# Two graph layers on one core: wider one-hot operations, a second product in halves, and a block transpose in place of a TensorE transpose

## The chip, the cores and the metric

The kernel runs on one core of one Trainium2 chip. The metric is the device time of one execution in microseconds (us). TensorE is PE in the profile, its weight loads are PEld, VectorE is DVE, ScalarE is ACT, GpSimd is POOL, and SyncE (SP) issues most DMAs.

## The reference, cut to what matters

There are 1250 nodes and 40000 edges, sorted by `dst`, with 512 features each.

```python
h = relu(layernorm(x))
msg = (h[src] + edge_attr) @ Wm.T + bm
agg = segment_sum(msg, dst) / max(deg, 1)
out = h + gelu(concat(h, agg) @ Wu.T + bu)
x = x + layernorm(out) * gamma + beta
h = relu(layernorm(x))
neigh = segment_sum(h[src], dst)
x = x + relu(((1 + eps) * h + neigh) @ W1 + b1) @ W2 + b2 + h
```

## The kernel before, in words

The sum over edges is made before the product with Wm. It has two parts: the sum of `edge_attr` rows per node, and the sum of `h[src]` per node, which is a product of h with a matrix of counts (how many edges go from node s to node d).

**The stream.** The 40000 edges are cut into 79 groups of 512 (NG = 79, the last has 64). SP loads each group (1 MB) into one of four buffers `ea` and reuses a buffer when `sums_done` says that the group's products are complete. Within a group there are two halves of 256 edges. As the edges are sorted, the nodes of a half lie in a window of W = 22 columns, whose first column is read at run time (`offsets`, two windows a group).

**Step n of the loop on PE** does, in this order: `sums(n)`, `turn(n-1)`, `counts(m)` for one or two groups m (`COUNTS`, four counts in three steps, so that all 79 are counted at step FULL = 58), then what `ASIDE` has for that step: a product of weights, a transpose of h0 (`T_AT`, one 128-row block each) or `u1` (`U_AT`, the product of a transposed block of h0 with Wu1T, four 128x512 matmuls in float32, which the profile shows as eight records). From step PIECE_AT = 60 on there is a `piece` in every step: eight matmuls of 512 columns that multiply the high part Hh and the low part Hl of h0 by a converted block of counts (ARc).

- `sums(n)` multiplies one-hot matrices oneD (512 edges by 22 columns) with `ea`. It uses four column groups of the PE array side by side: a 22-column weight sits at rows 0, 32, 64 or 96 of the output. It is 8 matmuls of 256 columns, 16 records.
- `turn(n)` transposes the packed sums. ACT copies them out of PSUM (`packed_copy`), PE transposes two blocks of 128x128, and the turned sums are then added into aggT. Before step EARLY = 59 ACT copies them again (`turned_copy`) and POOL adds (L400). From EARLY on DVE adds them straight from PSUM (L680).
- `counts(m)` multiplies the one-hot matrices oneS and oneK (bf16): four matmuls of 220 columns into one of two banks. DVE adds that bank into A16 (L669, `add_counts`, two halves). `counts(m)` waits until the adds of m-2 are complete.

**Step n on DVE** is an order written by hand: `sums_hots(n+2)` (oneD, two buffers, so it waits until `sums(n)` is complete), then for each counted group m: add of half 0, `key_hots(m+2)` (oneK, L648), add of half 1, `source_hots(m+2)` (oneS, L648). Then come the add of turned sums (from step 60 on), the drain of u1 (L688), folds of A16 (L698, steps 59 to 63), the degrees (step 66) and `has_bias` (steps 67 to 76). At step OUT_AT = 70 it drains the first ten pieces (`piece_out`, L720), and the eleventh piece on PE waits for that.

**POOL** adds the turned sums of groups 0 to 58 and makes the low part of h0, `low_h0` (L386: Hl = X - Hh), ten operations in steps T_AT + 2 (6 to 17). ACT makes the high part in the same steps (`HH_AT`). The first `piece` waits for all ten low parts.

After the loop come the rest of the pieces, `map_agg`, the first layer's normalisation, the second layer's products with the counts (L1171, L1172), the hidden layer (L1245) and the output (L1260). The change does not touch this part, except that the statistics of the second normalisation go to the array `stats` of the first.

Of the kernel before, what the change touches and what calls it, by code (L numbers as in the profile page):

```python
# [14 lines left out]
P = 128  # L15
SUB = 4
SLOTS = 4
HOTS = 2
# [9 lines left out]
def gnn_kernel(nc, x, src, dst, edge, Wm, bm, Wu, bu, gamma, beta, W1, b1, W2, b2, eps, out):  # L28
# [34 lines left out]
    assert len(ASIDE) == 4 + 2 * NT and U_AT[-1] < FULL and GEN_AT not in ASIDE and GEN_AT - 1 not in ASIDE  # L63
# [11 lines left out]
    DEG_BANK = 2 + (DEG_AT - 1) % 2  # L75
# [31 lines left out]

    stream_at = at[0]
    ea = [place(f"ea{s}", [P, SUB, D], F32)[0] for s in range(SLOTS)]
    oneD = [place(f"oneD{s}", [P, SUB, W], F32)[0] for s in range(HOTS)]  # L110
    oneS = [place(f"oneS{s}", [P, 2, P, 2], BF16)[0] for s in range(HOTS)]
    oneK = [place(f"oneK{s}", [P, 2, KW, 2], BF16)[0] for s in range(HOTS)]
    turned_sums = [place(f"turned_sums{s}", [P, D // 2], F32)[0] for s in range(HOTS)]
    packed_sums = [place(f"packed_sums{s}", [P, D // 2], F32)[0] for s in range(HOTS)]
# [5 lines left out]
    assert stream_at + NT * NP * 4 <= arc_at + NT * 256 * 4  # L120

    g_names = ["dst_f", "srel", "big", "valid", "hi_f", "lo_f", "key", "tmp"]
    dst_f, srel, big, valid, hi_f, lo_f, key, tmpf = [place("g_" + name, [P, GE], F32, arc_at + n * GE * 4)[0] for n, name in enumerate(g_names)]
    dst_i, _ = place("dst_i", [P, GE], I32, arc_at + 8 * GE * 4)
    src_i, _ = place("src_i", [P, GE], I32, arc_at + 9 * GE * 4)
    genE, _ = place("genE", [P, SUB, D], F32, arc_at)
    genD, _ = place("genD", [P, SUB, P], F32, arc_at + SUB * D * 4)
    genS, _ = place("genS", [P, SUB, P], BF16, arc_at + SUB * D * 4 + SUB * P * 4)
    genK, _ = place("genK", [P, SUB, P], BF16, arc_at + SUB * D * 4 + SUB * P * 6)

    idx_at = -(-at[0] // 32) * 32
    idxT = {n: place("T_" + n, [P, SUB, GP], F32)[0] for n in ("srel", "lo", "hi", "dE", "hit")}
# [3 lines left out]
    assert TB * 2048 <= 5 * SUB * GP * 4  # L136
    h0t = [place(f"h0t{i}", [P, D], F32)[0] for i in range(TB)]
    iotaF, _ = place("iotaF", [P, P], F32)
# [25 lines left out]
    stats2, _ = place("stats2", [P, NT, 6], F32)  # L164
# [12 lines left out]
    with ctx:  # L177
# [14 lines left out]
        counts_done = sem("counts_done")  # L192
        counts_zero = sem("counts_zero")
# [30 lines left out]
        turned_out = sem("turned_out")  # L224
# [17 lines left out]
        packed_out = sem("packed_out")  # L242
# [18 lines left out]
        turned = sem("turned")  # L261
        u1_done = sem("u1_done")
# [94 lines left out]
        def _(pool):  # L357
# [30 lines left out]
            def add_sums_of(n):  # L388
# [3 lines left out]
                for half, first in enumerate((loaded[0] & 0xFFFF, loaded[0] >> 16)):  # L392
# [6 lines left out]
                    sums = turned_sums[n % HOTS][:].rearrange("p (f q) -> p f q", f=FC)[:, :, half * QUAD:half * QUAD + W]  # L399
# [44 lines left out]
        def _(act):  # L444
# [62 lines left out]
            for n in range(NG):  # L507
                packed_copy(n)
# [26 lines left out]
            act.wait_ge(turned, NG)  # L535
# [54 lines left out]
        def _(dve):  # L590
# [45 lines left out]
            def sums_hots(n):  # L636
                if n >= HOTS:
                    dve.wait_ge(sums_done, n - HOTS + 1)
                n1 = idxT["srel"][:, :, n:n + 1].broadcast_to([P, SUB, W])
                V.tensor_tensor(oneD[n % HOTS][:], iotaF[:, 0:W].rearrange("p (a n) -> p a n", a=1).broadcast_to([P, SUB, W]), n1,  # L640
                                ALU.is_equal).then_inc(hotD_ready, 1)

            def counts_hots(m, hot, width, name, ready):
                if m >= HOTS:
                    dve.wait_ge(counts_done, m - HOTS + 1)
                iota = iotaP[:, 0:width].rearrange("p (a c) j -> p a c j", a=1).broadcast_to([P, 2, width, 2])
                mine = pairT[name][:, m].rearrange("p h (a j) -> p h a j", a=1).broadcast_to([P, 2, width, 2])
                V.tensor_tensor(hot[m % HOTS][:], iota, mine, ALU.is_equal).then_inc(ready, 1)  # L648

            def key_hots(m):  # L650
                counts_hots(m, oneK, KW, "key", hotK_ready)

            def source_hots(m):
                counts_hots(m, oneS, P, "lo", hotS_ready)
# [15 lines left out]

            def add_sums_of(n, half, first):
                cols = aggT[:, :, bass.ds(first, W)]
                if half == 0:
                    dve.wait_ge(turned, n + 1)
# [4 lines left out]
                sums = ps[:, 2 + n % 2, 0:256].rearrange("p (f q) -> p f q", f=FC)[:, :, half * QUAD:half * QUAD + W]  # L679
# [64 lines left out]
            for n in range(NG):  # L744
                if n + HOTS < NG:
                    sums_hots(n + HOTS)
# [541 lines left out]
```

## Time and profile before

| | us |
|---|---|
| three runs | 528.18, 529.69, 530.55 |
| median | 529.69 |
| the profiled execution, its own time | 526.39 |
| its span, first to last instruction | 524.6 |
| PE busy in the span | 482.8 (92%) |
| DVE busy | 283.0 (54%) |
| ACT busy | 147.5 (28%) |
| POOL busy | 166.8 (32%) |

Busy shares are means over stages that have different limits, so they are to be read stage by stage. All times below are from the start of the span. The loop's first `sums` starts at 27.75 us, and the loop's step 60, the first with a piece, begins at 208.53 us.

### The profile page before, as it was taken

The numbers are of one execution on the slowest core, as the hardware profiler recorded it, in microseconds if no ns is written. First come the engines' busy times: TensorE is split into PE (matmuls) and PEld (weight loads), VectorE is DVE, ScalarE is ACT, GpSimd is POOL, SyncE is SP. The second block draws the span as 40 slices with busy tenths as digits, with TensorE's granted clock in tenths as the row PEclk, the third lists the DMA queues.
The fourth block names the chain that finished last, engine by engine and source line by source line (L and its number), as shares of the span: only waits on it lengthen the run. The fifth ranks groups of instructions, "written<-read, shape, count | busy, mean of one in ns | idle before, by whom it ended". The sixth has DMA issues, their size and how long they took to land.

```text
span 524.6 us, 8826 instructions
## 1 busy us (share of the span) xinstructions
PE 482.8 (92%) x3003; PEld 277.0 (53%) x3003; DVE 283.0 (54%) x660; ACT 147.5 (28%) x291; POOL 166.8 (32%) x217
## 2 busy tenths in 40 slices
PE   5889999898898988999999999599989999999997
PEld 4446554444444544675665655379944446744442
DVE  6897887888777779645434789983000000011111
ACT  4416644123222223222237245441011122100000
POOL 7323665333322224000023267636994000000000
PEclk9999999999999999999999999799999999999999
DMA  8998998889999999988820111112040000011111
GB/s 299 316 367 301 338 327 292 348 342 361 352 367 358 374 363 390 408 308 315 271 82 2 32 29 41 35 62 100 1 163 0 0 0 1 0 41 40 41 40 35
DMA packets 31115, 98.95 MB, mean 189 GB/s; under 512 B 3577, under 2 KB 3577, under 8 KB 31067
## 3 DMA queue, kind: packets, MB, share of 16 engines
q1 hardware_dynamic: 30458, 97.27, 50.7%
q10 hardware_dynamic: 608, 1.05, 0.7%
q8 instruction: 28, 0.46, 0.4%
q14 instruction: 21, 0.16, 0.1%
HBM read 95.76 MB, written 2.56 MB: 187 GB/s over the span
## 4 chain that ended last, share of the span: by engine, by line
PE 63%; DVE 21%; issue 6%; PEld 6%; DVEq 1%; POOL 1%; DMA 1%; SPq 0%; PEldq 0%; POOLq 0%
PE ps L1260 13%; PE ps L1245 13%; PE ps L1007 9%; PE ps L1048 7%; DVE A L669 5%; PE ps L1105 5%; PE ps L1106 4%; PE ps L1018 4%; PE ps L1194 3%; PEld ps L1171 3%; PE ps L1036 3%; PEld ps L1172 2%; DVE U L893 2%; DVE tt L871 2%; DVE oneS L648 2%
## 5 line engine op out<-in xcount | busy, mean ns | idle before, releaser
L400 POOL TENSOR_TENSOR aggT<-turned_sums,aggT 128x88 f32 x118 | 53.9, 456 | 107.4 <-ACT turned_sums L473 94.4
L1007 PE MATMUL ps<-ea,oneD 128*22 128x256 f32 x1264 | 83.9, 383 | 1.4 <-DVE oneD L640 0.9
L947 DVE TENSOR_TENSOR U<-ps,U 128x512 f32<-128x512 f32 (+1 forms) x10 | 6.9, 692 | 130.8 <-PE ps L1260 130.8
L467 ACT COPY packed_sums<-ps 128x256 f32<-128x256 f32 x79 | 29.4, 372 | 163.9 <-PE ps L1007 163.9
L1245 PE MATMUL ps<-aggT,W1s 128*128 (+1 forms) x192 | 67.4, 513 | 2.2 <-PEq L1239 2.2
L1260 PE MATMUL ps<-W2s,hid 128*128 128x512 f32 (+1 forms) x160 | 68.8, 592 | 0.0
L669 DVE TENSOR_TENSOR A<-ps,A 128x220 f32 x158 | 60.3, 381 | 8.6 <-PE ps L1018 8.0
L1018 PE MATMUL ps<-oneK,oneS 128*128 128x220 bf16 x316 | 42.5, 259 | 14.7 <-DVE oneS L648 13.0
L1245 PEld LDWEIGHTS ps<-aggT,W1s 128*128 128x128 f32 x192 | 36.4, 190 | 33.1 <-issue 33.0
L1007 PEld LDWEIGHTS ps<-ea,oneD 128*22 128x22 f32 x1264 | 30.5, 101 | 41.1 <-issue 23.6
L648 DVE TENSOR_TENSOR oneK<-iotaP,P_key 128x880 bf16<-128x880 bf16 x79 | 51.8, 655 | 0.0
L1260 PEld LDWEIGHTS ps<-W2s,hid 128*128 128x128 f32 (+1 forms) x160 | 30.0, 188 | 38.2 <-issue 38.2
L1171 PE MATMUL ps<-AR,Hh 128*128 128x256 f32 (+1 forms) x160 | 45.2, 318 | 0.5
L1172 PE MATMUL ps<-AR,Hl 128*128 128x256 f32 (+1 forms) x160 | 44.0, 312 | 0.0
L640 DVE TENSOR_TENSOR oneD<-iotaF,T_srel 128x88 f32<-128x88 f32 x79 | 22.4, 283 | 37.0 <-PE ps L1007 35.8
L1018 PEld LDWEIGHTS ps<-oneK,oneS 128*128 128x128 bf16 x316 | 28.9, 97 | 21.2 <-DVE oneK L648 11.7
L648 DVE TENSOR_TENSOR oneS<-iotaP,P_lo 128x512 bf16<-128x512 bf16 x79 | 39.2, 496 | 0.0
L1194 PE MATMUL ps<-CT,aggT 128*128 128x512 f32 x80 | 36.0, 593 | 1.2 <-DVE aggT L720 1.2
L581 ACT ACTIVATE hid<-ps,b1C 128x512 f32 (+1 forms) x24 | 14.6, 608 | 80.3 <-PE ps L1245 80.3
L1048 PE MATMUL ps<-Wu1T,U 128*128 128x512 f32 x80 | 36.1, 593 | 0.0
L1036 PE MATMUL ps<-ident,packed_sums 128*128 128x128 f32 x158 | 34.5, 300 | 0.0
L1105 PE MATMUL ps<-ARc,Hh 128*128 128x512 f32 x80 | 33.4, 417 | 1.0 <-DVE aggT L720 1.0
(139 smaller groups left out, 645.1 us busy)
## 6 DMA issues: line engine op xcount, KB each, us to landing
ea<-in_edge_attr_dram SPq DMA_DIRECT2D x78, 1024.0 KB, 7.6
X<-in_x_dram SPq DMA_DIRECT2D x1, 2304.0 KB
xt<-in_x_dram SPq DMA_DIRECT2D x9, 256.0 KB, 2.7
out_dram<-U SPq DMA_DIRECT2D x9, 256.0 KB
W1s<-in_L_gnn_W_dram SPq DMA_DIRECT2D x1, 2048.0 KB, 7.7
W2s<-in_L_gnn_W_dram SPq DMA_DIRECT2D x1, 2048.0 KB, 8.7
WuN<-in_L_gnn_Wu_dram ACTq DMA_DIRECT2D x1, 1024.0 KB, 5.4
WuN<-in_L_gnn_Wu_dram SPq DMA_DIRECT2D x1, 1024.0 KB, 6.8
```

The lines of the kernel that those rows point to most:

```text
L400: nc.gpsimd.tensor_tensor(cols, sums, cols, ALU.add).then_inc(early_step, 1)
L648: V.tensor_tensor(hot[m % HOTS][:], iota, mine, ALU.is_equal).then_inc(ready, 1)
L669: V.tensor_tensor(cols, ps[:, 4 + m % 2, half * KW:(half + 1) * KW].rearrange("p (h w) -> p h w", w=W), cols, ALU.add).then_inc(add_step, 1)
L1007: last = T.matmul(to.rearrange("p (c d) -> p c d", c=2), oneD[h][:, g * 2 + j, :], data, start=j == 0, stop=j == 1)
L1018: last = T.matmul(ps[:, 4 + m % 2, (j // 2) * KW:(j // 2 + 1) * KW], oneS[h][:, j // 2, :, j % 2], oneK[h][:, j // 2, :, j % 2], start=j % ...
L1048: last = T.matmul(ps[:, ASIDE_BANK["u1", b], :], U[:, b, f * P:(f + 1) * P], Wu1T[:, f, :], start=f == 0, stop=f == FC - 1)
L1105: T.matmul(to, Hh[:, c, rows], counted, start=c == 0 and (q < 2 or f % 2 == 0), stop=False)
L1171: T.matmul(to, Hh[:, b, rows], AR[:, b, start:start + cols], start=b == 0 and (cols == 512 or f % 2 == 0), stop=False)
L1172: last = T.matmul(to, Hl[:, b, rows], AR[:, b, start:start + cols], start=False, stop=b == NT - 1 and (cols == 512 or f % 2 == 1))
L1194: last = T.matmul(ps[:, 2 + b % 2, :], aggT[:, f, b * P:(b + 1) * P], CT[:, f, :], start=f == 0, stop=f == FC - 1)
L1245: last = T.matmul(ps[:, CHUNK_BANK[k % 4], 0:cols], W1s[:, f, k * P:(k + 1) * P], aggT[:, f, bass.ds(start, cols)], start=f == 0, stop=f = ...
L1260: last = T.matmul(ps[0:rows, 6 + b % 2, :], hid[:, k, b * P:b * P + rows], W2s[:, k, :], start=k == 0, stop=k == KC - 1)
```

## The change

1. **u1 in two halves.** `u1(b)` makes its first two products at step U_AT[b] and the other two at the next step, and DVE drains it one step later. U_AT is 7, 12, 17, ..., 52 now; T_AT is more spread.
2. **One-hots of two groups per operation.** `pair_hots` makes oneK (and another one oneS) of the groups 2p and 2p+1 at once, in one of three pair buffers. At an even m the keys of the pair m//2 + 2 are made between the two adds, at an odd m the sources of that pair. oneD has three buffers, so `sums_hots(n+2)` in step n waits for `sums(n-1)` only.
3. **Low parts late.** `HH_AT` is 55 to 64 in place of 6 to 17, for ACT's high parts and POOL's low parts. A piece waits for its own low part alone.
4. **Block transposes.** From group EARLY = 59 on (20 groups) PE makes no `turn`, and ACT no `packed_copy`. `sums` puts each 32-column block of features where a transpose of 32x32 blocks turns it right: 16 matmuls of 128 columns in place of 8 of 256. DVE transposes the bank from PSUM to SBUF (`turn_blocks`, 128x256 float32) and then adds from SBUF. PE's `sums(n)` waits for `blocks_turned` of n-2. The products for the degrees come at step 65, after `sums`, and no longer inside `turn`.
5. Buffers are placed anew: two of the three pair buffers lie in the space of ARc, which is free until the counts are complete.

```diff
-HOTS = 2
+HOTS = 3
+SUM_HOTS = 3
+TURNS = 2
-    T_AT = [4, 5, 6, 8, 9, 10, 11, 13, 14, 15]
-    U_AT = [7, 12, 16, 21, 26, 32, 37, 42, 47, 52]
-    HH_AT = [t + 2 for t in T_AT]
+    T_AT = [4, 5, 6, 10, 11, 15, 16, 20, 21, 25]
+    U_AT = [7, 12, 17, 22, 27, 32, 37, 42, 47, 52]
+    HH_AT = [FULL - 3 + b for b in range(NT)]
...
+            def pair_hots(p, hot, width, name, ready):
+                if p >= HOTS:
+                    dve.wait_ge(counts_done, 2 * (p - HOTS + 1))
+                groups = min(2, NG - 2 * p)
+                halves_of = 2 * groups
+                iota = iotaP[:, 0:width].rearrange("p (a c) j -> p a c j", a=1).broadcast_to([P, halves_of, width, 2])
+                mine = pairT[name][:, 2 * p:2 * p + groups].rearrange("p g h (a j) -> p (g h) a j", a=1).broadcast_to([P, halves_of, width, 2])
+                V.tensor_tensor(hot[p % HOTS][:, 0:groups].rearrange("p g h c j -> p (g h) c j"), iota, mine, ALU.is_equal).then_inc(ready, 1)
...
+            def turn_blocks(n):
+                dve.wait_ge(sums_done, n + 1)
+                if n < TURNS + EARLY:
+                    dve.wait_ge(early_step, (n - TURNS + 1) * 2)
+                else:
+                    dve.wait_ge(sum_step, (n - TURNS + 1 - EARLY) * 2)
+                V.transpose(turned_sums[n % TURNS][:], ps[:, n % 2, 0:D // 2]).then_inc(blocks_turned, 1)
...
             for n in range(NG):
-                if n + HOTS < NG:
-                    sums_hots(n + HOTS)
                 if n > EARLY:
+                    turn_blocks(n - 1)
                     sum_first = offsets(n - 1)
+                if n > 0 and n - 1 + SUM_HOTS < NG:
+                    sums_hots(n - 1 + SUM_HOTS)
                 for m in COUNTS[n]:
                     first = count_first
                     add_counts(m, 0, first[0])
-                    if m + HOTS < NG:
-                        key_hots(m + HOTS)
+                    ahead = m // 2 + HOTS - 1
+                    if m % 2 == 0 and ahead < PAIRS:
+                        key_hots(ahead)
+                    elif ahead < PAIRS:
+                        source_hots(ahead)
                     if m + 1 < NG:
                         count_first = offsets(m + 1)
                     add_counts(m, 1, first[1])
-                    if m + HOTS < NG:
-                        source_hots(m + HOTS)
...
-                    elif kind == "u1":
-                        u1(k)
+                if n - 2 in U_AT:
+                    u1(U_AT.index(n - 2))
...
             def sums(n):
...
-                if n >= 2:
+                if 2 <= n < EARLY + 2:
                     pe.wait_ge(packed_out, n - 1)
+                elif n >= 2:
+                    pe.wait_ge(blocks_turned, n - 1 - EARLY)
...
+                else:
                     for g in range(2):
+                        for j in range(2):
+                            data = ea[s][:, g * 2 + j, :].rearrange("p (k q e) -> p q k e", k=FC, q=FC)
+                            for q in range(FC):
+                                to = ps[q * QUAD:q * QUAD + W, n % 2, g * P:(g + 1) * P]
+                                last = T.matmul(to.rearrange("p (k e) -> p k e", k=FC), oneD[h][:, g * 2 + j, :], data[:, q],
+                                                start=j == 0, stop=j == 1)
...
-                if n > 0:
+                if 0 < n <= EARLY:
                     turn(n - 1)
+                if n == DEG_AT - 1:
+                    degree_products()
                 for m in COUNTS[n]:
                     counts(m)
+                if n - 1 in U_AT:
+                    u1(U_AT.index(n - 1), 2)
```

## Rows read from the trace of the kernel before

**Rows 1.** Windows: span, then PE, PEld, DVE, ACT, POOL busy (x), clock, DMA share, GB/s

```profile
27.70:206.20 178.50, 161.99 (x1521) 84.78 (x1520) 148.59 (x400) 60.16 (x151) 67.49 (x125) 1.00 0.93 347
200.00:220.00 20.00, 18.14 (x183) 10.51 (x173) 16.20 (x42) 6.76 (x17) 3.93 (x9) 1.00 1.02 408
206.20:276.60 70.40, 67.33 (x544) 42.02 (x543) 35.50 (x93) 21.01 (x49) 6.44 (x8) 1.00 0.77 279
```

**Rows 2.** Chain of waits in the first stage: start us, us, what (x records)

```profile
174.75 3.45 PE ps L1048 x8
...
187.84 0.99 PE ps L1007 x16
188.84 0.37 PE ps L1036 x2
189.20 0.40 PE ps L1018 x4
189.60 3.45 PE ps L1048 x8
```

**Rows 3.** Waits in 60 to 200 us: total us, times, longest

```profile
DVE oneD L640 <- PE ps L1007: 17.1, 9, 2.6
...
PE ps L1018 <- DVE oneS L648: 10.6, 13, 1.4
PEld ps L1018 <- DVE oneK L648: 10.5, 9, 1.6
```

**Rows 4.** Timeline of DVE in a stretch where it has fallen behind: start us, us

```profile
121.07 0.39 DVE L669 TENSOR_TENSOR A<-ps,A 128x220 f32 x1
121.37 0.61 DVE L648 TENSOR_TENSOR oneK<-iotaP,P_key 128x880 bf16<-128x880 bf16 x1
...
122.19 0.42 DVE L648 TENSOR_TENSOR oneS<-iotaP,P_lo 128x512 bf16<-128x512 bf16 x1
122.52 0.69 DVE L688 TENSOR_TENSOR U<-ps,buB 128x512 f32<-128x512 f32 x1
```

**Rows 5.** A low part on POOL at 62.79 us, and DVE's one-hot beside it

```profile
62.79 1.26 POOL L386 TENSOR_TENSOR Hl<-X,Hh 128x512 fp32r<-128x512 f32 x1
...
62.85 1.49 DVE L648 TENSOR_TENSOR oneS<-iotaP,P_lo 128x512 bf16<-128x512 bf16 x1
```

**Rows 6.** The stream's loads: landing time, and issues on SP

```profile
DMA to landing us min/median/max: 2.3/7.6/13.6
...
SPq L312 <- PE ps L1007: 204.7, 74, 7.5
```

**Rows 7.** Chain of waits in the late steps, 239 to 251 us

```profile
240.69 0.37 PE ps L1036 x2
241.06 0.24 PE ps L1105
...
242.90 1.04 PE ps L1007 x16
...
243.97 0.25 DVE oneD L640
...
244.41 0.70 DVE aggT L720
...
247.68 0.99 PE ps L1007 x16
```

**Rows 8.** Weight loads by line, ns min/median/max; then one row of the chain

```profile
L1007 PEld LDWEIGHTS ps<-ea,oneD x1264: 97/102/103, 27.8 to 270.5; 128*22 128x22 f32 x181
...
L1018 PEld LDWEIGHTS ps<-oneK,oneS x316: 96/97/100, 28.7 to 205.9; 128*128 128x128 bf16 x158
...
67.18 0.44 PE ps L1042 x4
```

**Rows 9.** Timeline of DVE in a step with folds

```profile
212.87 0.25 DVE L640 TENSOR_TENSOR oneD<-iotaF,T_srel 128x88 f32<-128x88 f32 x1 [0.33 <-PE ps L1007]
213.47 0.25 DVE L680 TENSOR_TENSOR aggT<-ps,aggT 128x88 f32 x1 [0.36 <-PE ps L1036]
...
214.07 1.68 DVE L698 TENSOR_TENSOR acc<-acc,A 128x1280 uint16<-128x1280 uint16 x2
```

More of the change, by code:

```diff
@@ L62, in gnn_kernel @@
     GEN_AT = 29
-    assert len(ASIDE) == 4 + 2 * NT and U_AT[-1] < FULL and GEN_AT not in ASIDE and GEN_AT - 1 not in ASIDE
+    assert len(ASIDE) == 4 + 2 * NT and U_AT[-1] + 2 < FULL and GEN_AT not in ASIDE and GEN_AT - 1 not in ASIDE
     EARLY = FULL + 1
@@ L106, in gnn_kernel @@
     xt = [place(f"xt{i}", [P, D], F32, w1_at + i * 2048)[0] for i in range(TB)]
+    PAIRS = -(-NG // 2)
     stream_at = at[0]
     ea = [place(f"ea{s}", [P, SUB, D], F32)[0] for s in range(SLOTS)]
[L110 to L114, printed above, removed]
+    oneD = [place(f"oneD{s}", [P, SUB, W], F32)[0] for s in range(SUM_HOTS)]
+    packed_sums = [place(f"packed_sums{s}", [P, D // 2], F32)[0] for s in range(TURNS)]
+    turned_sums = [place(f"turned_sums{s}", [P, D // 2], F32)[0] for s in range(TURNS)]
+    oneK = [place("oneK0", [P, 2, 2, KW, 2], BF16)[0]]
     at[0] = -(-at[0] // 64) * 64
@@ L408, in _ @@
                         low_h0(b)
+            for b in range(NT):
+                if HH_AT[b] >= EARLY:
+                    low_h0(b)
             pool.wait_ge(low0_ready, NT)
@@ L723, in _ @@
             dve.wait_ge(consts, 3)
-            for n in range(HOTS):
+            for n in range(SUM_HOTS):
                 sums_hots(n)
-                key_hots(n)
-                source_hots(n)
+            for p in range(HOTS - 1):
+                key_hots(p)
+                source_hots(p)
             dve.wait_ge(x_in, 32)
@@ L825, in _ @@
                         V.nop()
+            turn_blocks(NG - 1)
             sum_first = offsets(NG - 1)
@@ L1009, in sums @@
                 last.then_inc(sums_done, 1)
             def counts(m):
-                h = m % HOTS
-                pe.wait_ge(hotK_ready, m + 1)
-                pe.wait_ge(hotS_ready, m + 1)
+                sources, keys = [t[m // 2 % HOTS][:, m % 2] for t in (oneS, oneK)]
+                pe.wait_ge(hotK_ready, m // 2 + 1)
+                pe.wait_ge(hotS_ready, m // 2 + 1)
                 if m >= 2:
@@ L1017, in counts @@
                 for j in range(SUB):
-                    last = T.matmul(ps[:, 4 + m % 2, (j // 2) * KW:(j // 2 + 1) * KW], oneS[h][:, j // 2, :, j % 2], oneK[h][:, j // 2, :, j % 2],
+                    last = T.matmul(ps[:, 4 + m % 2, (j // 2) * KW:(j // 2 + 1) * KW], sources[:, j // 2, :, j % 2], keys[:, j // 2, :, j % 2],
                                     start=j % 2 == 0, stop=j % 2 == 1)
@@ L1043, in transpose_h0, with u1 @@
                 last.then_inc(hT_mm, 1)
-            def u1(b):
+            def u1(b, first):
                 pe.wait_ge(hT_done, b + 1)
-                for f in range(FC):
+                for f in range(first, first + 2):
                     last = T.matmul(ps[:, ASIDE_BANK["u1", b], :], U[:, b, f * P:(f + 1) * P], Wu1T[:, f, :], start=f == 0, stop=f == FC - 1)
-                last.then_inc(u1_mm, 1)
+                if first == 2:
+                    last.then_inc(u1_mm, 1)
             def bank_free(what):
@@ L1103, in piece @@
                     to = bank("D", f, cols) if q == 2 else ps[:, 4 + f, 0:cols]
-                    counted = (ARd if q == 2 else ARc)[:, c, :]
-                    T.matmul(to, Hh[:, c, rows], counted, start=c == 0 and (q < 2 or f % 2 == 0), stop=False)
-                    last = T.matmul(to, Hl[:, c, rows], counted, start=False, stop=c == NT - 1 and (q < 2 or f % 2 == 1))
+                    here = (ARd if q == 2 else ARc)[:, c, :]
+                    T.matmul(to, Hh[:, c, rows], here, start=c == 0 and (q < 2 or f % 2 == 0), stop=False)
+                    last = T.matmul(to, Hl[:, c, rows], here, start=False, stop=c == NT - 1 and (q < 2 or f % 2 == 1))
                 last.then_inc(piece_mm, 1)
```

125 lines of the change are left out of this document (65 added, 60 removed).

## The prediction

> **What bounds the kernel now.** I read the windows first, to split the span into stages. The loop's steps 0 to 58 take the 178.5 us from 27.7 to 206.2, and the late steps, in which each has a piece, end at 276.6 [rows 1]. Behind 276.6 nothing of weight is changed. The reader is to see that no engine is full in the first stage: PE is busy for 162.0 us, DVE for 148.6, and the DMA moves 347 GB/s. In the late stage PE is busy for 67.3 of 70.4 us.
>
> Then the chain of waits gives PE's own price list [rows 2]: `sums` 0.99, `turn` 0.37, `counts` 0.40, `u1` 3.45, and a block's transposes 0.44 [rows 8]. The first stage by that list: 59 x 0.99 = 58.4, 58 x 0.37 = 21.5, 79 x 0.40 = 31.6, 10 x 3.45 = 34.5, two products of weights as long as a u1 = 6.9, ten transposes 4.4 and some 0.9 for two index tables: 158.2 us. So PE stands still for 20.3 of the 178.5 us. The waits name the cause: PE waits for oneS and oneK, 13 and 10 times in 140 us (10.6 and 10.5 us, partly the same time), while DVE for its part waits 17.1 us for `sums` [rows 3]. Two engines that wait for each other in turn are coupled too tightly. DVE waits while PE works off a u1 (between two u1 there are 14.85 us, from 174.75 to 189.60 [rows 2]), and then it is the slower one: a count costs it 1.45 us (121.07 to 122.52 [rows 4]), against 0.40 on PE.
>
> The loads are not the limit now: `ea` lands 7.6 us after issue in the median, SP spends 204.7 us waiting for a free buffer [rows 6], and PE never waits for `ea` [rows 3].
>
> **Early steps: u1 in halves, pairs.** Five steps hold one u1 and 6.67 counts. PE: 5 x (0.99 + 0.37) + 6.67 x 0.40 + 3.45 = 12.9 us, so of the 14.85 us 1.9 are stall. DVE: 6.67 x 1.45 = 9.7, 5 x 0.35 for oneD with its gap (0.25 [rows 9]) = 1.8, and the drain of u1 0.6: 12.1 us. In a step with one count DVE needs 1.8 us and PE 1.76, in one with two DVE 3.3 and PE 2.16. With 1.67 such steps, the drain and small change DVE falls back by some 2.8 us in five steps. A u1 gives it 3.45 us to catch up, but only a lag of about 1 us can be carried, since PE is never more than two counts ahead: the stall is 2.8 - 1.0 = 1.8, as measured. What does the change do to this?
> - Pairs. A key operation takes 0.52 us to the next start, a source operation 0.33 [rows 4], for 880 and 512 elements: 0.52 ns an element and 0.06 us fixed. A pair operation then takes 0.98 or 0.60 us, and saves 0.06. That is 0.12 us a pair, 0.4 us in five steps. With two counts in a step the add of the second now follows the add before it directly, with a gap of 0.18 as between two adds [rows 9]: 0.3 back. So pairs give DVE almost nothing.
> - Deeper buffers. A count on PE waits for the sources of m now, made directly after the add of m-2. It will wait for that add itself, which the code demands in both kernels. At even m the add now stands behind a key operation of 0.98 in place of 0.52, at odd m behind 0.60. Together no gain.
> - u1 in halves gives two breaks of 1.7 us, one step apart. The first takes up the lag carried, the second some of the next step's. I put the lag that is left over the other steps at 2.2 us, the stall at 1.2, and the gain at 0.7 us in five steps, 7 us over ten u1. The ends are 0, if two bursts so close act as one, and 1.9 x 10 = 19, if every stall goes.
>
> **Low parts.** A low part on POOL takes 1.26 us, and a one-hot that starts beside it takes 1.49 instead of 0.42 [rows 4, 5]: 1.07 us of DVE for each of ten, at most 10.7. They leave steps 6 to 17, where DVE is late anyway. I take 3 us of PE time (bounds 0, if other stalls take their place, and 6, a little over half of the 10.7). At the seam, PE begins step 60 at 208.53, 2.32 us after step 59 at 206.21, where its work is 1.36: DVE was late with oneD. The third oneD buffer takes this wait away, the conversion for the first piece stays behind the last count: 0.5 us. Early gain: 7 + 3 + 0.5 = 10.5 us.
>
> DMA: 10.5 us less in 59 steps is 2.85 us a step for 1.05 MB, 368 GB/s, and a window around the seam has 408 GB/s [rows 1], so I see no wait.
>
> **Late steps: the turn goes.** From the end of `sums` to the first piece there are 0.37 us (240.69 to 241.06 [rows 7]). Some of it is the way from packed to full-width matmuls and stays, so I take 0.28 a group. `sums` becomes eight rounds of 128 columns in place of four of 256. Four transposes of 128 columns take 0.44, 0.11 each [rows 8], and eight of those are 0.88, four rounds now take 0.99 with their start: I add 0.05. Net 0.23 x 20 = 4.6 us. The bounds of the round: it can't be shorter than now (0), and if each load of weights (0.102 us [rows 8]) had to end before the next round could stream, eight rounds would take 8 x 0.21 = 1.68, 0.7 more. I keep near the first: without overlap the four rounds of now would take 4 x (0.102 + 0.22) = 1.29, and 0.99 is measured.
>
> The Trainium skill says otherwise ("TensorE: Matmul & The Clock Gate", Part 3, The mechanism): weight loads overlap running matmuls only when the row group differs. Here all weights use all 128 rows, so by that rule nothing would overlap; the 0.99 us disagree with it at 256 columns, and no row shows 128 in column groups. By the rule the late steps would come out as in the second rival.
>
> Step 70: from 242.90 to 247.68 it takes 4.78 us, 1.57 more than the others (3.21), because `piece_out` (first at 244.41) starts only after the oneD operation at 243.97, which waits for that step's `sums` [rows 7]. With three buffers DVE starts about 1 us earlier: 1.0 us gained.
>
> **DVE in the late steps.** The block transpose isn't in the trace. Between 0.25 us for 88 columns and 0.69 for 512 [rows 4, 9] a line gives 0.42 for 256, and that is my value; bounds 0.25 and 1.0. In a fold step DVE has 0.42 + 0.25 + 0.50 + 1.68 and gaps of 0.4, 3.25 us, against PE's new 2.98. That makes it late by 1.4 us in five steps. Six low parts now fall into these steps and can block a fold each, 1.07 x 6 = 6.4 us. Behind the block transpose waits PE's `sums` of the next but one group: the leeway is two steps less one `sums`, 5.0 us. So up to 2.8 us of stall; I take 1.0, as low parts can meet idle time. With a transpose of 1.0 us it is up to 5.7. After step 64 DVE needs at most 0.42 + 0.25 + 0.50 + 0.7 + 0.4 = 2.3 us a step and is covered. ACT loses its copy. POOL ends its sums later by four low parts (5 us), and DVE's first add of its own waits for that, inside the same leeway.
>
> Late gain: 4.6 + 1.0 - 1.0 = 4.6 us.
>
> **The sum.** 10.5 + 4.6 = 15.1 us from 526.39, the profiled execution's own time (span 524.6 and 1.79 around it): 511.3. The median of the runs is 3.30 above that execution, and I keep the distance: 514.6.
>
> **The rivals.**
> - *Early steps hardly gain* (0.18). The add stands behind a longer operation and two bursts act as one: only the low parts and late steps pay, 3 + 0.5 + 4.6 = 8.1, so 522. For it: DVE's work per count is all but unchanged, 12.1 against 12.9 us. Against it: both have slack by that sum.
> - *Loads bind the narrow rounds* (0.10). 20 x 0.7 = 14 us against 5.6: late steps lose 8.5 to 9.5 us, with the early 10.5 it gives 528.5, no difference that can be told. Against it: the overlap seen now.
> - *Every stall goes* (0.06): 19 + 0.5 early, 4.6 late: 505.5. Against it: the loads would have to run at 1.05 MB in 2.7 us, 390 GB/s, with four buffers.
> - *Slower* (0.08): the pair operation with its four-part pattern runs at half the rate per element. Then a pair of groups costs 2784 x 0.52 = 1.45 us more on DVE, 4.8 us in five steps: DVE 16.9 us against the 14.85 of now, and the first stage is 2.05 x 12 = 24 us longer, 19 after the late gain: 544 to 549. It decides from about 0.85 ns an element on (0.4 us in five steps more than now would eat the late gain). Against it: the innermost pair of elements is laid out as before.
>
> **How the numbers follow.** The forecast has 0.58, with a range of its own from 508 to 520. A measurement here tells 0.5% (2.6 us) from no change. Faster: 0.58 + 0.18 + 0.06 = 0.82; same 0.10; slower 0.08. The range from 505 to 527.5 holds forecast and first rival, and most of the third, and leaves out some 2 in 10.
>
> **What would show it.** Right: waits of PE for one-hots fall from 20.3 us to about 10; one-hots last 1.07 and 0.69 us; no one-hot of 1.49 in steps 6 to 17; late steps 2.98 us apart; step 70 about 3.5; a block transpose of 0.42 us. Wrong: PE waits for the adds in L669's place as long as for one-hots before, rounds 0.2 us apart in `sums`, PE waiting for `blocks_turned` at steps 61 to 66, or PE waiting for `ea`.

## The result, and the profile after

The changed kernel takes 525.33 us (median of 20 runs, 522.43 to 528.55) against 527.89 (20 runs, 526.24 to 530.55). The ratio is 0.9955, with a 95% interval from 0.9938 to 0.9972. It is faster by 0.45%, some 2.4 us, where 15 were forecast. The time lies inside the stated range, but the gain is a sixth of the forecast. The two profiled executions, which all stretches below come from, took 526.39 and 525.55 us and differ by 0.8 us, the medians by 2.6.

The profile gives a span of 523.4 us. The windows of the kernel after, in the stretches of [rows 1]:

```profile
27.70:206.20 178.50, 166.82 (x1597) 87.65 (x1596) 141.89 (x333) 60.72 (x152) 69.89 (x123) 1.00 0.97 359
206.20:276.60 70.40, 65.98 (x757) 47.33 (x756) 48.88 (x107) 15.23 (x32) 17.02 (x13) 0.93 0.70 249
```

In the first stage PE does more in the same time (166.8 us of work against 162.0). In the second the granted clock is 0.93, where it was 1.00, POOL has 17 us of work in place of 6.4, and DVE 48.9 in place of 35.5.

To place the difference I took the start of each step, that is of its first `sums` record, from both traces (us):

| | before | after | after less before |
|---|---|---|---|
| step 0 | 27.75 | 29.45 | +1.70 |
| step 5 | 47.00 | 48.72 | +1.72 |
| step 21 | 97.47 | 93.96 | -3.51 |
| step 58 | 204.46 | 199.58 | -4.88 |
| step 63 | 218.15 | 219.24 | +1.09 |
| step 78 | 270.05 | 269.22 | -0.83 |
| `map_agg` | 276.64 | 274.92 | -1.72 |

At step 58 the new kernel is 4.9 us ahead, and five steps later 1.1 us behind. It loses 6.0 us between 199 and 219 us. The timeline of DVE and POOL there:

```profile
202.58 1.35 POOL L398 TENSOR_TENSOR Hl<-X,Hh 128x512 fp32r<-128x512 f32 x1
202.72 1.89 DVE L724 TENSOR_TENSOR acc<-A 128x1280 uint16<-128x1280 uint16 x1
...
205.45 0.44 DVE L695 STREAM_TRANSPOSE turned_sums<-ps 128x256 f32<-128x256 f32 x1
...
205.73 9.90 POOL L398 TENSOR_TENSOR Hl<-X,Hh 128x512 fp32r<-128x512 f32 x7
205.82 1.32 DVE L656 TENSOR_TENSOR oneD<-iotaF,T_srel 128x88 f32<-128x88 f32 x1
...
207.06 1.32 DVE L706 TENSOR_TENSOR aggT<-turned_sums,aggT 128x88 f32 x1
...
208.56 1.08 DVE L706 TENSOR_TENSOR aggT<-turned_sums,aggT 128x88 f32 x1 [0.18 <-DVE aggT L706]
...
209.56 3.70 DVE L724 TENSOR_TENSOR acc<-acc,A 128x1280 uint16<-128x1280 uint16 x2
...
213.19 0.44 DVE L695 STREAM_TRANSPOSE turned_sums<-ps 128x256 f32<-128x256 f32 x1
213.55 0.94 DVE L656 TENSOR_TENSOR oneD<-iotaF,T_srel 128x88 f32<-128x88 f32 x1
214.42 1.31 DVE L706 TENSOR_TENSOR aggT<-turned_sums,aggT 128x88 f32 x1
...
213.77 1.92 PE L1048 MATMUL ps<-ea,oneD 128*22 128x128 f32 x32 [3.72 <-DVE turned_sums L695]
```

POOL works off seven low parts without a break (9.90 us). Beside them the DVE operations with both inputs in SBUF are longer: oneD takes 1.32 us instead of 0.25, the two adds 1.32 and 1.08 instead of 0.25, two folds 3.70 instead of 1.68 [rows 9]. The block transpose, which reads PSUM alone, takes its 0.44. From one block transpose to the next pass 7.74 us, 5.0 of them lost beside POOL, and PE waits 3.72 us for the second. Within that wait, at about 212.2 us, the clock falls to 1.2 GHz. It stays there for 6.8 us, and the `sums` behind the wait takes 1.92 us where others take 1.07. The wait of 3.72 us and some 5.2 us of work at half clock, which is at most 2.6 us lost by estimate, make up nearly all of the 6.0 us (the turns that went give back 0.4).

### The profile page after: what moved, and what is told of

Its sections match the earlier page's. It is cut to its first block, busy times and chain, and to the rows that moved or that the text cites. A ratio compares the mean times of both kernels' runs of the same rounds, so it can differ in the third digit from the quotient of the medians.

```text
span 523.4 us, 9297 instructions
## 1 busy us (share of the span) xinstructions
PE 484.4 (93%) x3283; PEld 284.5 (54%) x3283; DVE 288.5 (55%) x602; ACT 140.9 (27%) x271; POOL 177.0 (34%) x217
## 4 chain that ended last, share of the span: by engine, by line
PE 65%; DVE 19%; issue 7%; PEld 6%; POOL 1%; DVEq 1%; DMA 1%; SPq 0%; PEldq 0%; POOLq 0%
PE ps L1305 13%; PE ps L1290 13%; PE ps L1040 7%; PE ps L1087 7%; PE ps L1146 5%; PE ps L1147 4%; PE ps L1059 4%; DVE A L687 4%; PE ps L1048 4%; PE ps L1239 3%; PEld ps L1215 3%; PE ps L1068 3%; PEld ps L1216 2%; DVE U L923 2%; DVE tt L901 2%
## 5 line engine op out<-in xcount | busy, mean ns | idle before, releaser
L412 POOL TENSOR_TENSOR aggT<-turned_sums,aggT 128x88 f32 x118 | 63.8, 541 | 101.3 <-ACT turned_sums L488 87.8
L687 DVE TENSOR_TENSOR A<-ps,A 128x220 f32 x158 | 60.7, 384 | 35.8 <-PE ps L1059 25.8
L1040 PE MATMUL ps<-ea,oneD 128*22 128x256 f32 x944 | 62.7, 383 | 0.1
L482 ACT COPY packed_sums<-ps 128x256 f32<-128x256 f32 x59 | 21.9, 372 | 113.5 <-PE ps L1040 113.3
L666 DVE TENSOR_TENSOR oneK<-iotaP,P_key 128x1760 bf16<-128x1760 bf16 (+1 forms) x40 | 42.6, 1066 | 0.0
L1040 PEld LDWEIGHTS ps<-ea,oneD 128*22 128x22 f32 x944 | 22.6, 101 | 35.2 <-issue 15.8
L1087 PE MATMUL ps<-Wu1T,U 128*128 128x512 f32 x80 | 37.8, 595 | 0.0
L1146 PE MATMUL ps<-ARc,Hh 128*128 128x512 f32 x80 | 35.4, 442 | 0.0
L1147 PE MATMUL ps<-ARc,Hl 128*128 128x512 f32 x80 | 33.1, 414 | 0.0
L1215 PEld LDWEIGHTS ps<-AR,Hh 128*128 128x128 f32 x160 | 31.0, 194 | 3.2 <-DVE Hl L944 1.3
L428 POOL TENSOR_TENSOR xt<-xt,betaB 128x512 f32<-128x512 f32 x10 | 14.3, 1429 | 52.7 <-DMA xt<-in_x_dram 52.5
```

Of the source, the lines that this page charges most:

```text
L412: nc.gpsimd.tensor_tensor(cols, sums, cols, ALU.add).then_inc(early_step, 1)
L687: V.tensor_tensor(cols, ps[:, 4 + m % 2, half * KW:(half + 1) * KW].rearrange("p (h w) -> p h w", w=W), cols, ALU.add).then_inc(add_step, 1)
L1040: last = T.matmul(to.rearrange("p (c d) -> p c d", c=2), oneD[h][:, g * 2 + j, :], data, start=j == 0, stop=j == 1)
L1087: last = T.matmul(ps[:, ASIDE_BANK["u1", b], :], U[:, b, f * P:(f + 1) * P], Wu1T[:, f, :], start=f == 0, stop=f == FC - 1)
L1146: T.matmul(to, Hh[:, c, rows], here, start=c == 0 and (q < 2 or f % 2 == 0), stop=False)
L1147: last = T.matmul(to, Hl[:, c, rows], here, start=False, stop=c == NT - 1 and (q < 2 or f % 2 == 1))
```

## The experiments

All but the changed kernel, whose row is the result above, were run in five rounds against the kernel before, which had 527.6 to 528.4 us there. The table gives the ratio to it (95% interval) and stretches of the profiled execution in us, between the starts of steps.

| kernel | us | ratio | steps 0-5 | 5-21 | 21-58 | 58-63 |
|---|---|---|---|---|---|---|
| before | | | 19.25 | 50.47 | 106.99 | 13.69 |
| changed | 525.33 | 0.9955 (0.9938 to 0.9972) | 19.27 | 45.24 | 105.62 | 19.67 |
| a_low_early | 521.40 | 0.9858 (0.9819 to 0.9898) | 20.82 | 46.03 | 105.49 | 13.72 |
| b_low_on_act | 518.35 | 0.9819 (0.9773 to 0.9865) | 19.13 | 45.24 | 104.63 | 13.86 |
| h_turn_psum | 523.87 | 0.9929 (0.9903 to 0.9955) | 19.30 | 45.24 | 105.62 | 16.62 |
| g_low_at_u1 | 521.54 | 0.9879 (0.9845 to 0.9914) | 19.65 | 46.02 | 108.06 | 13.51 |
| i_b_low_late | 523.43 | 0.9917 (0.9884 to 0.9949) | 19.38 | 45.56 | 108.37 | 14.10 |
| j_b_u1_halves | 523.94 | 0.9916 (0.9884 to 0.9948) | 18.33 | 46.15 | 108.05 | 13.44 |
| k_b_block_turn | 524.85 | 0.9942 (0.9916 to 0.9968) | 19.24 | 50.47 | 106.98 | 12.76 |
| l_u1_whole | 528.88 | 1.0013 (0.9985 to 1.0041) | 19.20 | 46.08 | 109.55 | 18.83 |
| m_no_pairs | 524.49 | 0.9944 (0.9918 to 0.9971) | 19.41 | 44.63 | 106.11 | 18.89 |
| n_low_early_start | 518.45 | 0.9815 (0.9788 to 0.9842) | 17.71 | 46.02 | 105.44 | 13.60 |
| p_low_on_dve | 516.17 | 0.9801 (0.9772 to 0.9831) | 17.65 | 45.24 | 104.68 | 12.81 |
| q_b_spread | 534.67 | 1.0142 (1.0118 to 1.0167) | 18.25 | 52.09 | 111.38 | 14.41 |

### Where are the 6 us of the seam?

**a_low_early**

```diff
-    HH_AT = [FULL - 3 + b for b in range(NT)]
+    HH_AT = [t + 2 for t in T_AT]
```

> The changed kernel with the low and high parts of h0 back in steps T_AT + 2 (6 to 27), nothing else. Seam theory: in the changed kernel the ten low parts run on POOL almost without a break from 197 to 216 us, in the steps in which DVE has the folds, and each blocks a DVE operation that reads two SBUF tensors (folds, oneD, the adds, which now read SBUF). PE then waits 3.7 us for a block transpose and its clock is halved for 6.8 us. With the low parts early the wait for blocks_turned and the slow clock at 212 us should be gone, the late steps start 5 to 6 us earlier, early steps lose 1 to 3 us: 521 to 523 us against 525.3. Rival (DVE is too full by the block transposes and the folds alone): the wait for blocks_turned stays above 2 us and the time is 525 to 528.

As expected, 521.40 us. Steps 58 to 63 fall from 19.67 to 13.72 us, and PE has no wait for a block transpose. So DVE is not too full by block transposes and folds alone, and the rival falls. What the early place costs is small: 0.8 us in steps 5 to 21.

**b_low_on_act**, which leaves out the subtraction of the low parts:

```diff
                 nc.scalar.copy(Hh[:, b, :], X[:, b, :]).then_inc(hi0_ready, 1)
+                act.wait_ge(hi0_ready, b + 1)
+                act.wait_ge(hT_mm, b + 1)
+                nc.scalar.activation(Hl[:, b, :], X[:, b, :], ACT.Copy, scale=0.0).then_inc(low0_ready, 1)
...
-                nc.gpsimd.tensor_tensor(Hl[:, b, :], X[:, b, :], Hh[:, b, :].bitcast(F32), ALU.subtract).then_inc(low0_ready, 1)
+                pool.wait_ge(low0_ready, b + 1)
```

> The changed kernel in which the low parts are made by ACT at the same late steps as 0 times X (this leaves the subtraction out, Hl becomes zero), so POOL and DVE don't meet there and all else keeps its place. Seam theory: no operation of DVE longer than its median between 197 and 216 us, no wait of PE for blocks_turned, full clock at 212 us: 6 us less than the changed kernel, 518.5 to 520. Rival (DVE too full by itself): within 1.5 us of the changed kernel's 525.3.

The seam takes 13.86 us with ten ACT operations in the same steps. DVE's timeline is even: a fold step takes 2.85 us (204.64 to 207.49) and nothing is stretched.

```profile
204.64 1.68 DVE L727 TENSOR_TENSOR acc<-acc,A 128x1280 uint16<-128x1280 uint16 x2
206.24 0.44 DVE L698 STREAM_TRANSPOSE turned_sums<-ps 128x256 f32<-128x256 f32 x1
206.60 0.21 DVE L659 TENSOR_TENSOR oneD<-iotaF,T_srel 128x88 f32<-128x88 f32 x1
206.89 0.25 DVE L709 TENSOR_TENSOR aggT<-turned_sums,aggT 128x88 f32 x1
...
207.49 1.68 DVE L727 TENSOR_TENSOR acc<-acc,A 128x1280 uint16<-128x1280 uint16 x2
```

The time, 518.35 us, is a little below what was expected. The cause is shown by this pair of runs: the late place alone costs nothing, it costs when POOL does the work beside these DVE operations. That Hl is zero in this run does not make the seam short, as a_low_early has the true low parts and the same 13.7 us.

**h_turn_psum** writes the block transpose to one PSUM bank, so it also waits for the adds of the group before:

```diff
...
-                V.transpose(turned_sums[n % TURNS][:], ps[:, n % 2, 0:D // 2]).then_inc(blocks_turned, 1)
+                V.transpose(ps[:, 3, 0:D // 2], ps[:, n % 2, 0:D // 2]).then_inc(blocks_turned, 1)
...
-                sums = turned_sums[n % TURNS][:].rearrange("p (h k w) -> p h k w", h=2, w=QUAD)[:, half, :, 0:W]
+                sums = ps[:, 3, 0:D // 2].rearrange("p (h k w) -> p h k w", h=2, w=QUAD)[:, half, :, 0:W]
```

> The changed kernel with the block transpose written to PSUM bank 3 instead of SBUF, so that the adds of the late groups read PSUM and SBUF as before the change. Seam theory in its fuller form: adds that read PSUM are not blocked by POOL (those of the counts never were, 373 to 393 ns), so at the seam only folds and oneD are: DVE regains the 3.0 us that three adds lost, and PE's wait falls from 3.7 to about 1: 522.5 to 524. If adds are blocked whatever they read, or the blocked folds alone decide, no difference: 525.3 within 1 us.

The time, 523.87 us, is as expected, but by the two intervals it can't be told from the changed kernel. What the run shows is in its profile. DVE's timeline:

```profile
205.69 1.31 DVE L656 TENSOR_TENSOR oneD<-iotaF,T_srel 128x88 f32<-128x88 f32 x1
206.93 0.24 DVE L706 TENSOR_TENSOR aggT<-ps,aggT 128x88 f32 x1
207.34 0.25 DVE L706 TENSOR_TENSOR aggT<-ps,aggT 128x88 f32 x1 [0.18 <-DVE aggT L706]
207.51 3.15 DVE L724 TENSOR_TENSOR acc<-acc,A 128x1280 uint16<-128x1280 uint16 x2
210.58 0.45 DVE L695 STREAM_TRANSPOSE ps<-ps 128x256 f32<-128x256 f32 x1
```

And its waits at the seam (total us, times, longest):

```profile
PE ps L1048 <- DVE ps L695: 3.4, 2, 1.8
```

The adds keep their 0.25 us beside running low parts, while oneD and folds are still stretched. The next block transpose starts at 210.58 instead of 213.19, and steps 58 to 63 shrink by 3.05 us. PE still waits 3.4 us for block transposes, but in two pieces, and no half clock follows. So about half the loss at the seam came from moving the source of the adds from PSUM to SBUF, together with the slow clock behind the long wait; this run does not separate the two.

**g_low_at_u1**

```diff
-    HH_AT = [FULL - 3 + b for b in range(NT)]
+    HH_AT = [u + 1 for u in U_AT]
```

> The changed kernel with one low part in each step U_AT + 1 (8, 13, ..., 53), where DVE has idle time while PE works off u1. Seam theory: the seam's 6 us come back, and the 1.07 us that each low part takes from a one-hot falls into DVE's idle time: 519 to 521 us. Rival (a low part costs its 1.07 us of DVE wherever it stands): ten of them cost the early steps what the seam gives back: 524 to 526.

The seam is clean (13.51 us), but steps 21 to 58 take 108.06 us against 105.62, and steps 5 to 21 0.8 us more. Against b_low_on_act steps 5 to 58 are 4.2 us longer, so a low part costs PE 0.4 us there, less than its 1.07 and not nothing. The time lies between the two expectations.

### What is each part worth by itself?

**i_b_low_late**: the kernel before with part 3 alone.

```diff
-    HH_AT = [t + 2 for t in T_AT]
+    HH_AT = [FULL - 3 + b for b in range(NT)]
...
-                    pe.wait_ge(low0_ready, NT)
+                if q == 0:
+                    pe.wait_ge(low0_ready, c + 1)
```

> The kernel before with the low and high parts of h0 moved to steps 55 to 64, nothing else. Seam theory: POOL's run of low parts blocks DVE's folds and oneD here too, but the late adds read PSUM and no product on PE waits for a block transpose, so only oneD (two buffers) can hold PE up: 1 to 3 us lost at the seam. The early steps gain about 0.5 us (what moving them back cost in the run before), more (up to 3 us) if they hurt more where u1 is whole. Time 526 to 530 against 527.6. Rival (the low parts cost nothing unless block transposes are there): 524 to 527.

Better than either theory had it. Steps 5 to 21 gain 4.9 us, steps 21 to 58 lose 1.4 (0.9 of them in steps 53 to 58, where the late low parts begin), and the seam only 0.4, although oneD and folds are stretched here too. The timeline of DVE shows the adds from PSUM at their full speed beside them:

```profile
211.04 1.33 DVE L643 TENSOR_TENSOR oneD<-iotaF,T_srel 128x88 f32<-128x88 f32 x1
212.30 0.24 DVE L683 TENSOR_TENSOR aggT<-ps,aggT 128x88 f32 x1
...
212.88 3.15 DVE L701 TENSOR_TENSOR acc<-acc,A 128x1280 uint16<-128x1280 uint16 x2
```

At the seam the late low parts hurt only where PE also waits for DVE's block transposes.

**j_b_u1_halves**: the kernel before with part 1 alone, **l_u1_whole**: the changed kernel without it, and **q_b_spread**: the kernel before with the new positions and whole u1.

```diff
-    T_AT = [4, 5, 6, 8, 9, 10, 11, 13, 14, 15]
-    U_AT = [7, 12, 16, 21, 26, 32, 37, 42, 47, 52]
+    T_AT = [4, 5, 6, 10, 11, 15, 16, 20, 21, 25]
+    U_AT = [7, 12, 17, 22, 27, 32, 37, 42, 47, 52]
...
-            def u1(b):
+            def u1(b, first):
                 pe.wait_ge(hT_done, b + 1)
-                for f in range(FC):
+                for f in range(first, first + 2):
```

(q_b_spread has the first four lines alone, l_u1_whole the whole edit in reverse.)

> The kernel before with u1 in halves and the new T_AT and U_AT, nothing else (low parts stay at T_AT + 2). If the halves make the early gain (as the prediction has it, 0.7 us in five steps), step 58 starts 5 to 7 us earlier than in the kernel before: 521 to 523 against 527.6. Rival (the halves need the deeper buffers for one-hots to be worth something): gain under 2 us.

> The changed kernel with u1 whole again and the old T_AT and U_AT (part 1 undone). If the halves make the early gain, step 58 starts 4 to 6 us later than in the changed kernel and the time is 529 to 531; the seam stays as it is in the changed kernel. Rival (pairs and deeper buffers make it): step 58 within 1.5 us of the changed kernel's, 525 to 527.

> The kernel before with the new T_AT and U_AT alone: transposes of h0, and with them the high and low parts (T_AT + 2), spread over steps 4 to 27, u1 whole. If the spread and not the halves made the gain of the kernel with both (523.94 us; steps 5 to 21 in 46.2 us against 50.5, steps 21 to 58 in 108.1 against 107.0), this one has 46 to 47 and 107.5 to 109: 524 us. Rival (the halves made it): 49.5 to 50.5 in steps 5 to 21, 526.5 to 528 us.

Halves with their new positions gain 4.4 us by the ratio, and taking both out of the changed kernel costs 3.1 (1.0013 against 0.9955; step 58 starts 4.65 us later). Both are more than the rivals allowed and a little less than was expected. q_b_spread refutes both its theories: with whole u1 the new positions are worse than the old, by 1.4%. Twice in the first stage of its trace the clock is at half, each time from within a wait of PE for oneS on. The rows are the two products that ended these waits, and the windows:

```profile
81.21 0.89 PE L1018 MATMUL ps<-oneK,oneS 128*128 128x220 bf16 x4 [2.59 <-DVE oneS L648]
132.26 0.89 PE L1018 MATMUL ps<-oneK,oneS 128*128 128x220 bf16 x4 [2.00 <-DVE oneS L648]
...
81.00:84.40 3.40, 3.19 (x24) 1.79 (x24) 3.36 (x10) 0.00 (x0) 0.31 (x1) 0.51 0.91 358
132.20:135.60 3.40, 3.34 (x24) 1.55 (x25) 2.83 (x8) 0.37 (x1) 0.00 (x0) 0.51 1.00 378
```

By estimate these cost at most 1.7 us each, half of 3.4. From q_b_spread to j_b_u1_halves steps 5 to 58 shrink by 9.3 us, up to 3.4 of them by the clock: by that the halves are worth about as much as I forecast (5.9 to 9.3 us against 7), and the new positions, with the clock that came with them, take back 6.0. In a stretch that neither positions nor low parts touch, steps 28 to 53 with five u1, the kernel before needs 73.29 us, halves alone 70.32, the changed kernel 70.48, and pairs with whole u1 (l_u1_whole) 75.39. So with whole u1 the pairs and deeper buffers cost 2.1 us there, and with halves nothing.

**k_b_block_turn**: the kernel before with part 4 alone.

```diff
-                if n > 0:
+                if 0 < n <= EARLY:
                     turn(n - 1)
...
+            def turn_blocks(n):
```

> The kernel before with the block transposes of the late groups alone (two oneD buffers, low parts early, u1 whole). By the after trace a late step is 0.145 us shorter: 20 x 0.145 = 2.9 us, and step 70 keeps its stall of 1.5 us, since the third oneD buffer is what takes it away: 524 to 525.5 against 527.6. Rival (DVE too full in the fold steps: its step can begin only when this step's sums are complete, 3.25 us of work against 3.06): 2 us of stall on PE at steps 60 to 65, 526 to 528.

As expected: 524.85 us, 0.9942, with no stall in the fold steps (12.76 us, the shortest seam) and the stall at step 70 unchanged (4.78 us).

**m_no_pairs**: the changed kernel with one-hots and buffers as before.

```diff
-HOTS = 3
-SUM_HOTS = 3
+HOTS = 2
...
-                pair_hots(p, oneK, KW, "key", hotK_ready)
+                counts_hots(m, oneK, KW, "key", hotK_ready)
```

> The changed kernel without part 2: one-hots of one group per operation in two buffers, two oneD buffers, as before; u1 halves, late low parts and block transposes stay. In the steps 21 to 58 the kernel before needs 107.0 us, halves alone 108.1, pairs with whole u1 109.5, both together 105.6. If only both together help, this one needs 107 to 108.5 there; step 70 has its stall of 1.5 us back; the start is 1.9 us earlier, since DVE has less to do before the statistics. Together 1 to 2 us slower than the changed kernel (525.3), 526 to 527.5. Rival (pairs and third buffers are worth nothing): 523 to 524.5.

The rival is right: 524.49, ratio 0.9944. Pairs and third buffers together are worth nothing that can be measured: steps 5 to 58 take 150.7 us without and 150.9 with them. They win the 1.5 us of step 70 (3.31 against 4.78 us) and lose it in the start.

### Two better versions

**n_low_early_start**

```diff
-    HH_AT = [FULL - 3 + b for b in range(NT)]
+    HH_AT = [t + 2 for t in T_AT]
...
-            for p in range(HOTS - 1):
-                key_hots(p)
-                source_hots(p)
+            key_hots(0)
+            source_hots(0)
...
-                    if m % 2 == 0 and ahead < PAIRS:
+                    if m < 2:
+                        key_hots(m + 1)
+                    elif m % 2 == 0 and ahead < PAIRS:
...
                     add_counts(m, 1, first[1])
+                    if m < 2:
+                        source_hots(m + 1)
```

> The changed kernel with the low and high parts at T_AT + 2 (521.4 us in its run) and, new, a shorter start: only the one-hots of the first pair are made before the statistics of x, those of pairs 1 and 2 beside the first two counts. Theory: the two pair operations and the statistics behind them hold up step 2 by 1.6 us (step 5 starts at 48.6 us against 47.0 before the change); that comes back, s5 at 47 and 520 us. Rival (the start is set by something else, as the adds of the first counts): step 5 within 0.4 us of 48.6 and the time as in that run.

Step 5 starts at 47.17 us instead of 48.6, and the time is 518.45, below the 520 that were expected. In the changed kernel the chain runs through four pair operations before the statistics of x:

```profile
23.22 0.98 DVE oneK L666
24.20 1.67 DVE oneS L666
25.88 1.40 DVE oneK L666
27.27 0.60 DVE oneS L666
27.88 5.95 DVE stats L757 x10
```

Before the change the statistics started at 25.75.

**p_low_on_dve** has the short start of the run before as well:

```diff
-    HH_AT = [FULL - 3 + b for b in range(NT)]
+    HH_AT = [u + 1 for u in U_AT]
...
+                if n in HH_AT:
+                    b = HH_AT.index(n)
+                    dve.wait_ge(hi0_ready, b + 1)
+                    dve.wait_ge(hT_mm, b + 1)
+                    V.tensor_tensor(Hl[:, b, :], X[:, b, :], Hh[:, b, :].bitcast(F32), ALU.subtract).then_inc(low0_ready, 1)
```

> The changed kernel with the short start and with the low parts made by DVE itself, one in each step U_AT + 1. DVE took 0.70 us for an operation of this shape later in the kernel (the second layer's low parts), less than the 1.07 us that it lost to each of POOL's. Theory: the stretch from the first sums to step 58, 173.7 us with POOL's low parts in these steps, falls to 170 to 171, the seam is clean: 517.5 to 519.5. Rival (any work on DVE in these steps costs PE as much): the stretch stays at 173 to 174 and the time at 521.

This has the lowest time: 516.17 us, 2.0% below the kernel before (1.7 to 2.3%) and below what was expected. The intervals of n_low_early_start and b_low_on_act overlap with its own, so only the stretches speak for it: against n_low_early_start steps 5 to 58 are 1.5 us shorter and steps 58 to 63 0.8. The groups of DVE, first stage:

```profile
L687 DVE TENSOR_TENSOR A<-ps,A 128x220 f32 x153 | 58.6, 383 | 28.8 <-PE ps L1067 19.3 <-DVE A L687 5.8 <-issue 1.0
...
L814 DVE TENSOR_TENSOR Hl<-X,Hh 128x512 fp32r<-128x512 f32 x10 | 6.8, 680 | 0.0
```

DVE makes a low part in 0.68 us, where POOL needs 1.26 and stops DVE for 1.07. First `sums` to step 58 takes 167.6 us.

## Why the prediction was wrong

**The step that failed** is in "DVE in the late steps": "So up to 2.8 us of stall; I take 1.0, as low parts can meet idle time." Steps 58 to 63 lost 6.0 us, where the forecast had a net loss of 0.5 (1.0 less the 0.5 gained with oneD). The mechanism was named, and so was its sign, PE waiting for `blocks_turned`. The time lost by DVE was also sized well: 6.4 us forecast, and between 205.8 and 216 us it adds up to some 6.7. Three things were wrong. The low parts were taken as spread over the steps, where idle time could take them up, but the code lets POOL make those of steps 59 to 64 one after another. Seven ran in one stretch, and 5.0 us of DVE were lost between two block transposes. A low part was let block "a fold each", but oneD and the two adds, which part 4 moves from PSUM to SBUF, were stretched as well, so that no idle time was left between them; h_turn_psum shows the adds' part. Together that is a wait of 3.72 us where 1.0 was taken and 2.8 was the bound. And there was no term for the clock, which fell to half for 6.8 us within that wait. a_low_early and b_low_on_act show that nothing else was lost there.

**The start.** The prediction gave it no term. Four pair operations before the statistics made step 5 1.7 us late; n_low_early_start gives 1.4 back. In the changed kernel's profile the clock is also halved around 21 us, but a_low_early has full clock there and the same late step 5, so the order on DVE decides.

**Early steps.** Forecast 10 us up to step 58, measured 6.6 from step 5 on. By parts: the halves were put at 0.7 us in five steps, and steps 28 to 53 show 0.56 to 0.59, with halves alone as well as in the changed kernel. The size was nearly right, but it was applied to all ten u1, and the new positions in steps 5 to 28 cost something by themselves, which had no term (q_b_spread). Low parts were put at 3 us: in their early place they cost 1.7 us from step 5 to 58 against a kernel without any on POOL (a_low_early and b_low_on_act). In the kernel before, where u1 is whole, moving them is worth 4.9 us in steps 5 to 21 and 3.5 up to step 58 (i_b_low_late). These terms don't add: moving the low parts or halving u1 each gain 4 to 5 us in steps 5 to 21 by themselves, and both together 5.2 to 5.8.

**Pairs.** "Almost nothing" was right, with its prices: 1.065 and 0.682 us against 1.07 and 0.69. That refutes the rival of a pair operation at half the rate. The waits changed their name as said (whole span, total us, times, longest):

```profile
DVE A L687 <- PE ps L1059: 25.8, 21, 2.4
...
PE ps L1059 <- DVE A L687: 10.1, 14, 1.6
PEld ps L1040 <- DVE oneD L656: 8.0, 14, 0.8
...
PEld ps L1059 <- DVE oneK L666: 6.3, 8, 1.8
```

PE now waits for adds, 14 times, and DVE 25.8 us for counts. The two still wait for each other. Between 60 and 200 us the waits for adds are 8.5 us, not much less than the 10.6 for oneS before, and the prediction had named that as a sign of being wrong. So the rival "every stall goes" falls, but not by the loads that were held against it: PE waits for none of them between 60 and 200 us.

**The turn.** Forecast 0.23 us a step, measured 0.142 (3.207 to 3.065). The rounds were right: eight rounds 0.109 us apart, with loads of 0.102 us beside the running rounds. That refutes the second rival. It also disagrees with the sentence of the Trainium skill ("TensorE: Matmul & The Clock Gate", Part 3, The mechanism) that loads overlap with running matmuls only when the row group differs. The same section also lets a load into the background weight buffer go ahead; the traces do not tell whether that is what happens here. The weight loads by line:

```profile
L1048 PEld LDWEIGHTS ps<-ea,oneD x640: 97/102/163, 201.3 to 269.9; 128*22 128x22 f32 x160
```

And the timeline of a late step:

```profile
253.90 1.07 PE L1048 MATMUL ps<-ea,oneD 128*22 128x128 f32 x32
254.91 0.50 PE L1146 MATMUL ps<-ARc,Hh 128*128 128x512 f32 x1
255.25 0.39 PE L1147 MATMUL ps<-ARc,Hl 128*128 128x512 f32 x1
```

What was mis-sized is the share of the 0.37 us that stays. That figure runs from the end of `sums` to the end of the turn, and the next product had begun long before. The same stretch of the kernel before:

```profile
236.42 1.06 PE L1007 MATMUL ps<-ea,oneD 128*22 128x256 f32 x16
237.41 0.44 PE L1036 MATMUL ps<-ident,packed_sums 128*128 128x128 f32 x2
237.61 0.48 PE L1105 MATMUL ps<-ARc,Hh 128*128 128x512 f32 x1
237.93 0.40 PE L1106 MATMUL ps<-ARc,Hl 128*128 128x512 f32 x1
```

From the start of the turn to the start of the piece there are only 0.20 us, and no more than that could go. From the start of `sums` to the first piece there were 1.19 us and are 1.01 now, 0.18 less. The piece takes 0.04 more, from its start to the next `sums` (2.06 us against 2.02). So 0.18 was gained where 0.28 less 0.05 was forecast. Step 70 gained 1.46 us (1.0 forecast). The block transpose took 0.446 us (0.42).

**In sum**, up to `map_agg`, forecast and measured: start 0 and +1.7; steps 5 to 58 -10.0 and -6.6; seam +0.5 and +6.0; turns and step 70 -5.6 and -4.3, and +1.5 for a stretch of half clock at the degree products (step 65), which had no term. Together -15.1 and -1.7. The forecast also kept the 3.30 us by which the median of three runs lay above the profiled execution. That was chance: the median of the 20 runs before is 1.50 above it, and that of the changed kernel lies 0.22 below its own profiled execution.

## What to carry to other kernels

When work is moved from POOL to a quieter place, list which DVE operations there read two SBUF tensors; each may wait for a whole POOL operation, and an add that is switched from a PSUM to an SBUF source joins them. A dependency that runs through the engine which is stretched turns a harmless contention into a stall: here late low parts alone gained, block transposes alone gained, and together they lost 6 us at the seam. Gains from two edits that relieve the same stretch are not to be summed; make each edit alone first.

## What the runs showed of the hardware

- DVE operations with both inputs in SBUF were stretched by up to 1.07 us beside a POOL operation of 1.26 us (oneD 0.25 to 1.32, an add 0.25 to 1.32), in float32 as well as in 16-bit. The same add from PSUM kept 0.24 to 0.25 us beside the same POOL operations (h_turn_psum, i_b_low_late). The Trainium skill ("SBUF — State Buffer", SBUF: two separate sides) says that a DVE operation with two SBUF inputs and a GpSimd operation that reads SBUF exclude each other for the whole instruction; the traces agree.
- PE's clock fell to 1.2 GHz in the middle of the loop: for 6.8 us from within the wait of 3.72 us on, for 3.4 us from within waits of 2.59 and 2.00 us (q_b_spread), and for 3.4 us behind the 20 one-column products of step 65 (2.29 us). The window 229.0 to 232.6 has a mean clock of 0.55, and there a float32r matmul of 512 columns follows the last in 0.43 instead of 0.23 us. The kernel before, with the same 20 products, kept its clock there in the profiled execution, as did four of the experiments (h_turn_psum, g_low_at_u1, i_b_low_late, l_u1_whole). What sets it off is open. The first row is the window from within the wait on, the second the one behind the products:

```profile
212.10:218.90 6.80, 5.13 (x40) 3.96 (x40) 6.33 (x11) 0.44 (x1) 3.52 (x3) 0.51 0.67 232
...
229.00:232.60 3.60, 3.60 (x27) 2.38 (x29) 0.60 (x5) 0.62 (x1) 0.00 (x0) 0.55 0.50 205
```

- Column-packed products of 128 columns in float32 ran in rounds of four every 0.109 us, 14 ns for a weight load or a matmul. Rounds of 256 columns took 0.216 us, so twice as many instructions for the same columns cost no more than 0.01 us a group.
